# Attention and routed feed-forward on one core: when the table of routed rows is cleared, in which packets, and from which period on probabilities are moved by DMA

## The reference

```python
x = x + attention(layernorm(x), ctx)      # 16 batches of 256 rows of 256; ctx 16 x 256 x 192
x = x + routed_ffn(layernorm(x))
# attention: 16 heads of 64
q, k, v = xn @ w_q, ctx @ w_k, ctx @ w_v
attn = softmax(q @ k.T * 64 ** -0.5)
out = (attn @ v) @ w_o + b_o
# routed_ffn: 8 experts, top 2, at most 640 rows for each expert, 4096 tokens
gates = softmax(x @ router_w + router_b)
pos = cumsum(expert_mask) - 1             # a token's slot in each of its experts
buf[e, pos] = x                           # rows over the capacity are dropped
out = gelu(buf @ w1[e] + b1[e]) @ w2[e] + b2[e]
y[n] = sum over e of gates[n, e] * out[e, pos[n, e]]
```

## Time and profile before

| | |
|---|---|
| median of 3 runs | 913.05 us (910.46 to 913.29) |
| the profiled execution | 914.2 us, its span 912.4 us |
| busy PE / DVE / ACT / POOL | 882.8 / 727.7 / 535.9 / 403.2 us |
| granted TensorE clock over the span | 0.99 |
| DMA packets | 154427, 180.94 MB |

### The profile page before, as it was taken

The page is one execution under the profiler, slowest core; times in us unless marked ns, Lnnn a source line. Parts: engine busy times, 40 slices in busy tenths (PEclk is TensorE's granted clock), DMA queues, the critical chain, the costliest instruction groups (busy, mean ns, idle before and its releaser), DMA issues.

```text
span 912.4 us, 21639 instructions
## 1 busy us (share of the span) xinstructions
PE 882.8 (97%) x7552; PEld 781.9 (86%) x7552; DVE 727.7 (80%) x1580; ACT 535.9 (59%) x1535; POOL 403.2 (44%) x622
## 2 busy tenths in 40 slices
PE   7999999999999999999999999997899999999995
PEld 7877888888888888888888888886799999999995
DVE  5776789898988989898998988986877787668762
ACT  5875676676766676676676766765443354334520
POOL 5553435545464554646545465433333222332223
PEclk9999999999999999999999999999999999999998
DMA  8577888888888878888788888777239556554322
GB/s 234 154 224 242 257 239 257 235 251 239 259 250 245 262 218 258 253 246 269 220 244 254 237 244 251 227 213 223 82 112 198 101 100 146 132 134 64 97 29 29
DMA packets 154427, 180.94 MB, mean 198 GB/s; under 512 B 62300, under 2 KB 127946, under 8 KB 150480
## 3 DMA queue, kind: packets, MB, share of 16 engines
q1 hardware_dynamic: 128784, 143.97, 53.6%
q10 hardware_dynamic: 16704, 26.62, 11.2%
q0 software_dynamic: 8832, 8.98, 5.8%
HBM read 106.00 MB, written 78.47 MB: 202 GB/s over the span
## 4 chain that ended last, share of the span: by engine, by line
PE 72%; DVE 10%; DMA 8%; ACT 5%; issue 2%; SPq 1%; ACTq 0%; POOLq 0%; POOL 0%; DVEq 0%
PE psum L814 21%; PE psum L1082 10%; PE psum L1066 10%; PE psum L925 10%; PE psum L881 8%; PE psum L941 8%; DMA squares<-prob 4%; ACT prob L1154 3%; DVE hidl L1302 2%; DVE prob L1385 2%; DMA inverses<-invturned 1%; PE psum L904 1%; DVE bufl L1302 1%; DMA invrows<-inverses 1%; DMA probt<-squares 1%
## 5 line engine op out<-in xcount | busy, mean ns | idle before, releaser
L1154 ACT ACTIVATE prob<-psum,negmax 128x256 f32<-128x256 f32 x512 | 239.2, 485 | 122.5 <-DVE negmax L1356 105.4
L1356 DVE TENSOR_REDUCE negmax<-psum 128x2 f32<-128x512 f32 x256 | 158.4, 681 | 35.6 <-PE psum L881 35.4
L684 POOL TENSOR_TENSOR al<-attended,ah 128x512 fp32r<-128x512 f32 x57 | 73.7, 1292 | 193.8 <-ACT ah L1093 193.7
L790 POOL DMA_INDIRECT out_rows<-y,rowi x40 | 66.3, 1658 | 159.0 <-DVE y L1614 135.6
L1385 DVE STREAM_TRANSPOSE prob<-prob 128x1024 f32<-128x1024 f32 x116 | 127.5, 1099 | 6.1 <-ACT prob L1154 5.9
L925 PE MATMUL psum<-probt,v 128*64 128x256 f32 x1024 | 126.0, 389 | 1.9 <-DMA probt<-squares 1.9
L1274 ACT ACTIVATE hid<-psum,b1t 128x640 f32<-128x640 f32 x64 | 50.9, 796 | 126.6 <-PE psum L1066 126.6
L1154 ACT ACTIVATION_READ_ACCUMULATOR prob<-psum,negmax 128x1 f32 x512 | 111.0, 217 | 0.0
L925 PEld LDWEIGHTS psum<-probt,v 128*64 128x64 f32 x1024 | 68.5, 137 | 39.6 <-issue 7.3
L1082 PE MATMUL psum<-w2h,hidh 128*128 128x256 f32 x320 | 91.2, 285 | 1.4 <-DVE hidl L1302 1.4
L1082 PE MATMUL psum<-w2l,hidh 128*128 128x256 f32 x320 | 90.5, 283 | 0.0
(11 more groups left out here) (212 smaller groups left out, 2602.8 us busy)
## 6 DMA issues: line engine op xcount, KB each, us to landing
squares<-prob SPq DMA_DIRECT2D x29, 1024.0 KB, 4.8
squares<-prob SPq DMA_DIRECT2D x29, 768.0 KB, 6.2
invrows<-inverses SPq DMA_DIRECT2D x128, 128.0 KB, 4.0
probt<-squares SPq DMA_DIRECT2D x58, 256.0 KB, 5.0
probt<-squares ACTq DMA_DIRECT2D x58, 256.0 KB, 5.8
probt<-squares SPq DMA_DIRECT2D x58, 192.0 KB, 3.8
probt<-squares ACTq DMA_DIRECT2D x58, 192.0 KB, 4.4
w1r<-in_w SPq DMA_DIRECT2D x8, 1024.0 KB, 5.2
```

Of the source, the lines that this page charges most:

```text
L684: pool.tensor_tensor(al[:, b % 2, c:c + 2, :], attended[:, :, :], ah[:, b % 2, c:c + 2, :].bitcast(F32), ALU.subtract).then_inc(sem("a_lo" ...
L790: pool.indirect_dma_start(out=out_rows, out_offset=bass.IndirectOffsetOnAxis(ap=rowi[:, e % 2, s:s + 1], axis=0), in_=y[:, e % 2, s, :], i ...
L1154: last = act.activation(into, out_of, ACT.Exp, bias=negmax[:, m % 2, u, qb:qb + 1], accum_out=total[:, m % 2, u, qb:qb + 1])
L1356: dve.tensor_reduce(negmax[:, m % 2, u, :], psum[:, u, :].rearrange("p (q s) -> p q s", q=ST), AX.X, ALU.max, negate=True).then_inc(sem("m ...
```

## The change

There are three edits. `MOVED` begins at period 2 instead of 4, so the heads of periods 2 and 3 are transposed by squares and DMA (three heads of period 2, four of period 3), and the fourth PSUM bank joins the rotation two periods earlier. All nine clearing DMAs are issued in period 1, between `inv_out(0)` and `inv_in(0)`, instead of three each at the ends of periods 2, 3 and 4, and GpSimd's `constants` goes from period 2 to behind the first `vsplit`. The third edit is in `clear`: a partition writes five neighbouring rows, 5 x 1060 bytes in one piece, instead of rows that lie 128 apart; the numbers of the spare rows in `dumpi` follow suit. One line keeps `a_lo` of the first periods in place, which the other form of a period would leave out.

```diff
--- before.py
+++ after.py
@@ -62,7 +62,7 @@
 
 
 
-MOVED = range(4, PERIODS - 2)
+MOVED = range(2, PERIODS - 2)
 WHOLE = (1, 3)
 
 POOL_REST = range(PER_B - 1, PERIODS - 4)
@@ -101,7 +101,7 @@
     out = steps("ln1_stats ln1_root ctx ln1", 0) + steps("split_hi split_lo", 0) + steps("split_hi split_lo", 1)
     out += [("warm", 28), *steps(xt, 0), ("warm", 8)]
     out += steps("split_hi split_lo", 2) + steps("split_hi split_lo", 3) + steps(q, 0) + steps(k, 0)
-    out += [*steps("q q_hi", 1), ("vsplit", 0), ("ctx", 1), *steps("scores max0 max1 exp0", 0), ("q_lo", 1),
+    out += [*steps("q q_hi", 1), ("vsplit", 0), ("constants", 0), ("ctx", 1), *steps("scores max0 max1 exp0", 0), ("q_lo", 1),
             *steps("max2 max3", 0), ("split_hi", 4), *steps(k, 1), ("exp1", 0), ("split_lo", 4),
             *steps("exp2 exp3 v v_sb", 0), ("split_hi", 5)]
     for m in range(1, PERIODS - 2):
@@ -156,6 +156,7 @@
             out += [("x2add", ST * (b - 2) + 1)] if r == 1 and 2 <= b else []
             out += [("bias", b - 3)] if r == 0 and 3 <= b else []
             out += [("q_lo", m + 1), ("square0", m), ("k_lo", m + 1), ("square1", m), ("a_norm", m - 2)]
+            out += [("a_lo", m - 2)] if m - 2 < POOL_REST[0] else []
         out += [("square1", m)] if four and m in MOVED else []
         if r == 0:
             out += steps("shift compare rank", b - 3) if 3 <= b else []
@@ -171,7 +172,7 @@
 
         out += {1: [("ln1_root", 1)]}.get(m, [])
         out += [("ctx", b + 1)] if r == 2 and 1 <= b < B - 1 else []
-        out += {1: [("vsplit", 1)], 2: [("constants", 0)], 3: [("residual", 0), ("residual", 1)], 4: [("vsplit", 2)],
+        out += {1: [("vsplit", 1)], 3: [("residual", 0), ("residual", 1)], 4: [("vsplit", 2)],
                 5: [("vsplit", 3)]}.get(m, [])
         out += [("scatter", b - 4)] if r == 0 and 4 <= b else []
         out += [("a_lo", m - 2)] if m - 2 in POOL_REST else []
@@ -183,10 +184,10 @@
 
         out += [("load_ctx", 2)] if m == 2 else []
         out += ([("move_low", m - 1)] if m - 1 in MOVED else []) + [("inv_out", m - 1)]
+        out += [("clear", third) for third in range(3)] if m == 1 else []
         out += ([("lift", m)] if m in MOVED else []) + [("inv_in", m - 1)]
         out += [("traffic", b - 2)] if r == 1 and 2 <= b else []
         out += [("load_ctx", b + 2)] if r == 3 and 1 <= b < B - 2 else []
-        out += {2: steps("clear", 0), 3: steps("clear", 1), 4: steps("clear", 2)}.get(m, [])
 
 
     c, d, e, m, z = B - 3, B - 2, B - 1, PERIODS - 2, PERIODS - 1
@@ -511,10 +512,10 @@
             def clear(third):
                 sp.wait_ge(sem("blank"), 1)
                 for e in range(3 * third, min(3 * third + 3, NE)):
-                    sp.dma_start(table[e * CAP:(e + 1) * CAP, :].rearrange("(s p) w -> p s w", p=P),
+                    sp.dma_start(table[e * CAP:(e + 1) * CAP, :].rearrange("(p s) w -> p s w", p=P),
                                  blank[:, :, :]).then_inc(sem("table_clear"), 16)
                 if third == 2:
-                    sp.dma_start(out_rows[N:N + CAP, :].rearrange("(s p) w -> p s w", p=P),
+                    sp.dma_start(out_rows[N:N + CAP, :].rearrange("(p s) w -> p s w", p=P),
                                  blank[:, :, 0:D]).then_inc(sem("spare_clear"), 16)
 
             def inv_out(m):
@@ -720,7 +721,7 @@
                 link(pool.affine_select(out=lower[:, :, :], in_=lower[:, :, :], compare_op=ALU.is_gt, fill=0.0,
                                         base=0, pattern=[[1, NE], [-1, NE]], channel_multiplier=0))
                 link(pool.iota(slot0i[:, :], pattern=[[CAP, NE]], base=-1, channel_multiplier=0))
-                link(pool.iota(dumpi[:, :], pattern=[[P, ET]], base=N, channel_multiplier=1))
+                link(pool.iota(dumpi[:, :], pattern=[[1, ET]], base=N, channel_multiplier=ET))
                 link(pool.iota(toki[:, :], pattern=[[P, ST]], base=0, channel_multiplier=1))
                 link(pool.tensor_copy(slot0[:, :], slot0i[:, :]))
                 link(pool.tensor_copy(tok[:, :], toki[:, :]))
```

## The result

The changed kernel takes 919.3 us (median of 5 runs, 919.25 to 922.43) against 913.05 us (5 runs, 910.46 to 913.62): a ratio of 1.0074, 95% interval 1.0052 to 1.0096, so 6.3 us slower. A second series of the same kernel gave 1.0071 (1.0047 to 1.0094). Its profiled execution has a span of 919.3 us (921.1 in all), 6.9 more than the one of before.

The account below looks back on a forecast made before the run. The prediction took TensorE as the bound, busy in 97% of the span, so early losses pass almost undiminished to the end. +11.7 + 1.8 - 4.2 - 3.7 = +5.6 us on the 913.05 us median gave 918.7, range 913 to 926.

Parts of the forecast that it names:

- A: The forecast case, chance 0.80: reciprocals of the first period wait behind all clears; 918.7 us, own range 915.9 to 924.1.
- Constants earlier on GpSimd: GpSimd's 4.2 us constants block, put before `ctx(1)`, hides in an idle gap: cost nothing, at most 4.2 us of GpSimd.
- `inv_in(0)` behind all clears: Period 1, SyncE's queue: reciprocals' load lands after all clears, so `a_norm(0)` starts at 44.5 instead of 32.75, +11.7 us.
- Who waits: Period 2: TensorE stops before `v(2)` for 9 us until `a_norm(0)` is done; `scores(3)` is 11.7 us late.
- Clock: After TensorE's 9 us idle the granted clock falls to half: +1.8 us, low end 0.5, high end 3.5.
- Periods 2 and 3 moved: Periods starting with `scores(3)` and `scores(4)` shorten to 8.13 and 7.69 us without TensorE transposes: together -4.2 us.
- The stall at 74 us: With no clears ahead of its move, the wait before `pv(4)` goes: 14.23 - 10.55, -3.7 us.
- The sum: +11.7 + 1.8 - 4.2 - 3.7 = +5.6 us, put on the median: 918.7 us.
- B: Rival, chance 0.12: small transfer `inv_in(0)` isn't held by the clears, `a_norm(0)` 3.9 us late; -4.0 us, 909.1 us.
- Case C: Rival, chance 0.08: nearly no change, clears written faster or stall taken up later by unseen idle; 913 to 914.4 us.

Follow-up runs that it names:

- clears alone: Changed kernel, but heads moved only from period 4 on, as before: 924.2 us, ratio 1.013 to the kernel before.
- four ahead: Changed kernel, heads moved from period 4 on, four clears ahead of `inv_in(0)`, four ending period 2, spare rows ending period 3: 917.4 us, ratio 1.0063.
- small packets: Changed kernel with the old layout of the clears, packets of 1060 bytes instead of 5300: 926.5 us, ratio 1.0163.
- second profile: The changed kernel run once more, nothing changed: 921.8 us beside 914.7, ratio 1.0071.
- the best version: Changed kernel, but five clears behind `inv_in(0)` in period 1, then one ending each of periods 2 to 5: 912.7 us, ratio 0.9966.
- the clears in the empty stretch alone: Changed kernel, moved from period 4, four clears ending periods 1 and 2, behind `inv_in(0)`: 912.9 us, ratio 1.001; again 915.3 us, 0.9999.

## Why the prediction was right, and which terms were off

The forecast was +5.6 us, 918.7, within 913 to 926; measured 919.3. The likeliest case, A, is what happened, and the runs with clears alone, four ahead and small packets show its cause.

*Constants earlier on GpSimd.* Forecast nothing. They ran from 15.56 to 20.6, 5.1 us for 4.2, and `ctx(1)` started at 20.73, 0.35 later than before; TensorE did not wait for it. Whether their traffic makes the early fall of the clock likelier is open: of the 12 profiles with the constants in the new place six have it, of the two without none. In the changed kernel it would hide behind the stop.

*`inv_in(0)` behind all clears.* The mechanism was right, the term too small: 11.7 us forecast, 13.1 measured (45.84 - 32.75), 13.8 in the second profile. From the first clear's issue to `a_norm(0)` I had 1.6 + 13.3 + 2.1 + 0.8 = 17.8 us, and it is 19.4. The rate of the pieces was nearly right, 400 for 407, worth 0.3 us. The nine issues took 9.5 us where I had 6.2, since from the third on a clear took 0.9 to 1.3 us to issue and not 0.6; that made `inv_in(0)` go out at 35.98 and not at 33, still before the data ahead of it were through. What was mis-sized is the end of the block. I gave the spare rows and `inv_in(0)` 2.9 us for 0.92 MB at 318 GB/s and no time to land. From 41 to 45 us the engines are full at 287 GB/s, with the loads of `ctx(2)`, issued right behind, among the packets:

```profile
41.00:45.00 4.00, 0.00 (x0) 0.00 (x0) 0.00 (x0) 0.00 (x0) 0.00 (x0) 0.70 1.01 287
```

With four pieces ahead the same fixed part is 37.44 - 27.03 - 6.8 = 3.6 us where the sum had 2.4: about a microsecond was missing there as well. That it is time to land is my reading. The times of landing only place it: the last table piece landed at 43.7, where the sum had 41.6, the spare rows at 44.9 for 43.7, and `inv_in(0)` 0.9 us behind them for 0.8. So the time was lost ahead of the landing of the spare rows, not behind it.

*Who waits.* Right in each step: TensorE stopped at `v(2)`, 9.1 us for 9, and `scores(3)` followed 6.1 us behind the end of `a_norm(0)` (46.5 to 52.67; 6.0 forecast).

*Clock.* +1.8 forecast. It fell twice, during the stop (0.81 from 42 to 43 us, then 0.50 until 49) and again after the 1.91 us of idle time before `xt(1)` at 51.68:

```profile
46.00:49.00 3.00, 2.41 (x6) 1.82 (x7) 2.62 (x6) 2.43 (x8) 0.00 (x0) 0.50 0.04 5
53.50:55.50 2.00, 2.00 (x21) 1.78 (x17) 1.97 (x7) 0.28 (x1) 0.72 (x2) 0.50 0.60 169
```

The first fall cost nothing to speak of: from `a_norm(0)` to `scores(3)` it took 6.1 us, and 6.0 at full clock before. The second cost 9.61 - 8.12 = 1.5 us: in the second profile the same period ran at full clock in 8.12. There TensorE had idled 1.74 us in the same place, and the clock did not fall. So the term was near by luck: the fall that I had argued from cost nothing, and the one that cost something comes in one profile and not in the other.

*Periods 2 and 3 moved.* -4.2 forecast. At full clock the first takes 8.12 (second profile) and the second 7.69 (first profile), forecast were 8.13 and 7.69. In the second profile the second one is 9.0, with 1.3 us of idle time ahead of `scores(5)`, so a part of this gain isn't always there. And the condition for it was missing from the forecast: no clear lies in these periods. The moved periods alone, with clears among them, lost 7 to 8 us.

*The stall at 74 us.* -3.7 forecast, 14.23 - 10.57 = 3.7 measured.

*The sum.* In the profile 13.3 - 2.7 - 3.7 = 6.9 where I had 11.7 + 1.8 - 4.2 - 3.7 = 5.6; `scores(3)` is 1.6 us later than forecast, 1.4 of it by `a_norm(0)`, and the periods behind it give back 0.3 more. Medians differ by 6.3, nearer to the forecast than its terms were. In the second profile `scores(3)` is 14.0 late and `scores(7)` 7.7, and the span is only 5.3 longer. Of the 2.4 us between, 2.0 are the one wait late in the kernel, at the passage to the experts, which is not constant; waits of TensorE from 600 to 700 us, before, changed kernel, and its second profile:

```profile
PE psum L904 <- ACT probt L1093: 5.3, 1, 5.3
```

```profile
PE psum L905 <- ACT probt L1094: 4.8, 1, 4.8
```

```profile
PE psum L905 <- ACT probt L1094: 3.3, 1, 3.3
```

5.3, 4.8 and 3.3 us. The sum took the passage to the end as one to one. In these traces it is so to 2 or 3 us, and single executions differ by as much.

*The rivals.* B, that the small transfer finds its way between the large ones, is excluded by `a_norm(0)` at 37.44, 45.84 and 50.48 for four pieces, nine, and nine in small packets. The rule of the Trainium skill that each DMA engine consumes its ring in order ("DMA: Bandwidth & Descriptors", section "Queues, rings and completion order") agrees with these traces, with 8.5 us to landing for 3.1. It is not the whole of it, since a write of 16 KB took 11.4 us with the clears on another queue. The limit of about 358 GB/s for HBM that the same page of the Trainium skill gives (section "Where 436 GB/s comes from") did not hold the clears back in this program of one core: they ran at 400. Case C did not occur.

## What to carry to other kernels

Price a DMA by the bytes that were issued ahead of it and have not landed, with their measured rate, and count those of other queues too, and add about 3 us in all for issue and landing, which is what was left over here. A block of bulk writes between the two halves of a small round trip costs its whole length; the same block behind the second half left the kernel here level with the one before instead of 6 us slower. Then price the block a second time by the share of the DMA engines that the periods around it leave free, since another queue gave no relief here. That bulk belongs in the periods with idle engines, in pieces no longer than the slack of the next small transfer, is what the best version suggests, with 0.34% to show for it; the clears in the empty stretch alone gained nothing.

## What the runs showed of the hardware that I had not expected

- Writes of 5300 bytes per partition in one packet ran at 400 GB/s, nearly the rate of a lift with 6 KB packets (407), and writes of five rows of 1060 bytes at 313. The share of the DMA engines was 1.02 and 1.06.
- GpSimd's queue gave no relief. With clears there, 36 to 52 us moved 383 GB/s at a share of 1.01, and TensorE's stop was 3.61 us, with the clears on SyncE's queue 3.01. A write of 16 KB on SyncE's queue took 11.4 us to land.
- The granted clock fell to 0.50 during an idle time of 9.11 us and again after one of 1.91 us; in the second profile of the same kernel it fell during 10.60 us and not after 1.74. It also fell in six of 14 profiles near 22 us, though the program up to there was the same as in six others that kept the full clock, and TensorE was busy for 1.74 or 1.75 of the 2.5 us before in all 14.
